# A decoder layer of attention, retention and mixture of experts: the weighing, the maxima and a quarter of the K projection at other places in the step

## The reference

```
x = layernorm(x + attention(x, Wqkv))         # 16 heads of 16, causal
x = layernorm(x + retention(x, ctx, Wq,Wk,Wv)) # xpos rotation, decay mask, no softmax
x = layernorm(x + moe(x))                      # one shared expert + top 2 of 8
```

## Time and profile before

| | us |
|---|---|
| median of 3 runs | 827.55 |
| lowest, highest | 826.76, 829.4 |
| the profiled execution, its own time | 829.99 |
| its span, first to last instruction | 828.2 |
| PE busy | 727.1 (88%) |
| DVE, ACT, POOL busy | 443.5, 385.3, 320.3 |
| K projection on PE | from 5.59 to 35.09 |
| scores of tile 0 start | 38.91 |
| steps 4 to 30, start of scores to start of scores of step 31 | 91.10 to 444.94 |
| first expert tile's transpose | 519.74 |

### The profile page before, as it was taken

The page is one execution under the profiler, slowest core; times in us unless marked ns, Lnnn a source line. Parts: engine busy times, 40 slices in busy tenths (PEclk is TensorE's granted clock), DMA queues, the critical chain, the costliest instruction groups (busy, mean ns, idle before and its releaser), DMA issues.

```text
span 828.2 us, 20209 instructions
## 1 busy us (share of the span) xinstructions
PE 727.1 (88%) x5972; PEld 539.4 (65%) x5973; DVE 443.5 (54%) x1506; ACT 385.3 (47%) x1105; POOL 320.3 (39%) x451
## 2 busy tenths in 40 slices
PE   7966898988989898898988864899999999999894
PEld 6745687877878787787877741466666666665453
DVE  3513555656556555656556563344444444446985
ACT  0055666766667666666667220233333333321333
POOL 1001222323443444444344666255555555550010
PEclk9969999999999999999999997899999999999998
DMA  8718441221322323232232545342222222227872
GB/s 306 260 31 241 148 134 52 67 77 52 92 78 79 95 62 103 67 90 77 79 98 81 173 123 181 99 145 85 87 83 89 84 88 83 89 70 253 283 257 77
DMA packets 77035, 97.69 MB, mean 118 GB/s; under 512 B 12320, under 2 KB 63264, under 8 KB 75936
## 3 DMA queue, kind: packets, MB, share of 16 engines
q1 hardware_dynamic: 59920, 68.31, 26.9%
q0 software_dynamic: 6816, 19.00, 6.5%
q10 hardware_dynamic: 10224, 9.42, 4.4%
HBM read 60.12 MB, written 36.56 MB: 117 GB/s over the span
## 4 chain that ended last, share of the span: by engine, by line
PE 71%; issue 12%; ACT 5%; DVE 4%; DMA 3%; POOL 3%; SPq 1%; ACTq 0%; POOLq 0%; DVEq 0%
PE ps L977 15%; PE ps L779 7%; PE ps L988 7%; ACT prob L1066 4%; PE ps L767 4%; PE ps L742 4%; PE ps L717 4%; PE ps L854 4%; PE ps L867 4%; PE ps L870 3%; PE ps L793 3%; PE ps L745 3%; PE ps L963 2%; PE ps L970 2%; PE ps L841 2%
## 5 line engine op out<-in xcount | busy, mean ns | idle before, releaser
L1066 ACT ACTIVATE prob<-ps,nmax 128x128 f32<-128x128 f32 x512 | 146.3, 377 | 2.6 <-DVE nmax L1229 1.8
L977 PE MATMUL ps<-first_use,xgT 128*128 x284 | 135.4, 600 | 1.5 <-ACT xgT L1163 1.5
L1229 DVE TENSOR_REDUCE nmax<-ps 128x4 f32<-128x512 f32 x128 | 86.3, 683 | 93.1 <-PE ps L767 93.1
L621 POOL TENSOR_TENSOR rot<-products 128x128 f32<-128x128 f32 x128 | 59.0, 481 | 186.9 <-DVE products L1239 186.9
L1073 ACT COPY pT<-ps 128x512 f32<-128x512 f32 x128 | 75.0, 586 | 88.0 <-PE ps L779 82.4
L1452 DVE TENSOR_TENSOR hid<-ps,attn_only 128x512 f32<-128x512 f32 x71 | 49.1, 692 | 101.6 <-PE ps L977 100.5
L1163 ACT COPY xgT<-ps 128x256 f32<-128x256 f32 x71 | 26.4, 372 | 140.9 <-PE ps L963 140.9
L670 POOL TENSOR_TENSOR gate_h<-hid,sil 128x256 f32<-128x256 f32 x71 | 50.7, 715 | 96.2 <-DVE result_row L1465 82.7
L779 PE MATMUL ps<-tf,prob 128*128 128x128 f32 x512 | 84.1, 289 | 3.3 <-ACT pT L1073 3.3
L1239 DVE TENSOR_TENSOR products<-ps,tf 128x256 f32<-128x256 f32 x128 | 48.4, 420 | 61.5 <-PE ps L870 44.1
L977 PEld LDWEIGHTS ps<-first_use,xgT 128*128 128x128 f32 x284 | 54.3, 192 | 40.4 <-issue 36.9
(11 more groups left out here) (133 smaller groups left out, 1352.5 us busy)
## 6 DMA issues: line engine op xcount, KB each, us to landing
xg<-sent ACTq DMA_DIRECT2D x68, 129.5 KB, 2.1
first_use<-back SPq DMA_DIRECT2D x8, 1024.0 KB, 8.2
k_dram<-first_use SPq DMA_DIRECT2D x4, 1024.0 KB, 6.0
attn_only<-in_x_turned SPq DMA_DIRECT2D x32, 128.0 KB
attn_only<-k_dram SPq DMA_DIRECT2D x256, 16.0 KB
attn_only<-in_x SPq DMA_DIRECT2D x32, 128.0 KB, 2.3
first_use<-in_L_ffn_rw SPq DMA_DIRECT2D x8, 512.0 KB, 5.7
attn_only<-in_ctx SPq DMA_DIRECT2D x32, 128.0 KB, 2.2
```

Source lines behind the costliest of these rows:

```text
L621: eng.tensor_tensor(rot[:, t % 2, m + e, :], ra[:, t % 2, m + e, :], rb[:, t % 2, m + 1 - e, :], ALU.add).then_inc(done, 1)
L977: mm = eng.matmul(ps[:, r, :], xgT[:, r, c, :], rw1_sb[:, bass.ds(e * (DC * 2 * FFN) + c * 2 * FFN, 2 * FFN)], start=(c == 0), stop=(c == ...
L1066: ins = eng.activation(prob[:, t % 2, 4 * u + n, :], SCORE[u][:, n * P:(n + 1) * P], ACT.Exp, bias=nmax[:, t % 2, 4 * u + n:4 * u + n + 1])
L1229: eng.tensor_reduce(nmax[:, t % 2, 4 * u:4 * u + 4], SCORE[u].rearrange("p (h j) -> p h j", j=P), AX_X, ALU.max, negate=True).then_inc(max ...
```

## The change

The eight weighing matmuls of each half become one block of 16 for tile n-2 at the start of step n, ahead of the scores. DVE takes all four maxima first and all of the gating last in its step; ACT's exponentials stand earlier, and the masks are laid last in PE's step, behind the x1 transposes. The retention's K and V come before its Q, SCX moves to bank 7 and YX behind the x2 transposes. POOL's step begins with x2b and the sends. Group 3 of the K projection moves into step 0 (three units) and step 1 (the fourth), with DVE's copies and SP's stores; SP waits only for the first store before it loads K. The weight loads begin at step 3. The diff, cut (repeated lines of moved blocks are left out):

```diff
-MAX_ORDER = (3, 0, 2, 1)
+MAX_ORDER = (3, 0, 1, 2)
...
-    return GROUPS[q][0] + GROUPS[q][1] + 5
+    return GROUPS[q][0] + GROUPS[q][1] + 4
...
-            if group_step(q) + 3 + (j if size == 4 else 0) == n]
+            if group_step(q) + 4 + (j if size == 4 else 0) == n]
...
-        SCX = ps[:, 6, 0:P]
+        SCX = ps[:, 7, 0:P]
...
-            for g in range(NG - 1):
-                store_k(g)
-
-            eng.wait_ge(k_stored[0], 16)
+            store_k(0)
...
                     if t < 2:
                         eng.wait_ge(consts_set, 2)
+                    if t == 0:
+                        eng.wait_ge(k_stored[0], 16)
...
-                    store_k(NG - 1)
-                if n == 1:
+                if n in (-1, 0, 1):
+                    store_k(n + 2)
+                if n == 3:
                     eng.wait_ge(k_stored[1], 16 * (NG - 1))
-                if 1 < n <= 1 + NE // 2:
+                if 2 < n <= 2 + NE // 2:
...
-                    for e in range(2 * (n - 2), 2 * (n - 1)):
+                    for e in range(2 * (n - 3), 2 * (n - 2)):
...
             def step(n):
-                t = n - 3
-                if live(t):
-                    turn_into(t, 2, pq_set, rot_q_set)
-                    turn_into(t, 0, pk_set, rot_k_set)
...
                 if n == 2:
                     eng.wait_ge(zeros_set, 1)
                     eng.dma_start(sent[IDLE_ROW:XROWS, :].rearrange("(n p) d -> p n d", p=P),
...
+                t = n - 5
+                if live(t):
+                    eng.wait_ge(x2_set, t + 1)
...
+                    eng.tensor_tensor(x2b[:, t % 2, :], packets[:, t % SLOTS, 0:D], sb2_sb[:, :], ALU.add).then_inc(x2b_set, 1)
                 for t in sent_at(n):
                     eng.wait_ge(pos_set, group_of(t) + 1)
                     for j in range(TOPK):
...
+                t = n - 3
+                if live(t):
+                    turn_into(t, 0, pk_set, rot_k_set)
+                    turn_into(t, 2, pq_set, rot_q_set)
...
+            def project_k(g, j, bank):
...
+                mm.then_inc(k_made, 1)
+            for g in range(NG - 1):
+                eng.wait_ge(xTu_in[g] if g else wk_in, 16)
+                    project_k(g, j, 4 + j)
+            eng.wait_ge(xTu_in[NG - 1], 16)
...
-            eng.wait_ge(kk_set, 4 * NG - 2)
+            eng.wait_ge(kk_set, 4 * NG - 5)
...
-                if t < 5:
+                if t < 4:
                     after(eng, q_set, t)
+                if t == 4:
+                    eng.wait_ge(pq_set, 2)
...
-            def weigh(t, u0):
-
-                eng.wait_ge(pT_set, t * 4 + u0 + 2)
...
+            def weigh(t):
+
+                eng.wait_ge(pT_set, t * 4 + 4)
+                eng.wait_ge(v_set, t + 1)
+                after(eng, att_set, t)
+                for h in range(H):
+                    lo = h % CG * VW
+                    mm = eng.matmul(HEADS_T[lo:lo + VW, h // CG, :], va[:, t % 3, h, :],
+                                    pT[:, h % 8 // 2, 2 * (h // 8) + h % 2, :], start=True, stop=True)
                 mm.then_inc(heads_made, 1)
...
+            def bank7_read(n):
+
+                eng.wait_ge(gc_set, min(n - 5, B))
+                for q in groups_at(n - 1, 3):
+                    eng.wait_ge(base_set, q + 2)
             def step(n):
-                if n == -1:
+                if n == 2:
                     eng.wait_ge(kk_set, 4 * NG)
+                if live(n - 2):
+                    weigh(n - 2)
                 if live(n):
                     scores(n)
+                if n == 0:
+                    eng.wait_ge(kk_set, 9)
+                    project_k(NG - 1, 0, 4)
+                if n == 1:
+                    eng.wait_ge(kk_set, 13)
                 if live(n - 1):
                     turn_probs(n - 1, 0)
+                if n == 1:
+                    eng.wait_ge(kk_set, 14)
+                    project_k(NG - 1, 3, 5)
+                t = n - 3
+                if live(t):
+
+                    eng.wait_ge(cT_in[t % 2], t // 2 * 16 + 16)
+                    eng.wait_ge(x1T_set, t + 1)
+                    for q in groups_at(n - 1, 3):
+                        eng.wait_ge(base_set, q + 2)
+                    for m in range(2):
+                        for c in range(DC):
...
+                    for c in range(DC):
+                        mm = eng.matmul(XV, cT[:, t % 2, c, :], xwv_sb[:, c, :], start=(c == 0), stop=(c == DC - 1))
+                    mm.then_inc(xkv_made, 1)
                 t = n - 2
                 if live(t):
 
@@ -840,10 +864,11 @@
                     for b in range(H // CG):
...
                     mm.then_inc(heads_turned, 1)
+                if live(n - 1):
+                    turn_probs(n - 1, 1)
                 t = n - 3
                 if live(t):
 
-                    eng.wait_ge(x1T_set, t + 1)
...
-                if live(n - 1):
-                    turn_probs(n - 1, 1)
...
-                if live(n - 1):
-                    turn_probs(n - 1, 2)
                 t = n - 4
                 if live(t):
...
                     if live(n - 3):
-                        eng.wait_ge(pq_set, 2 * (n - 3) + 2)
+                        eng.wait_ge(pk_set, 2 * (n - 3) + 2)
                     else:
-                        eng.wait_ge(res2_set, n - 4)
+                        bank7_read(n)
                     for m in range(2):
...
                     mm.then_inc(scx_made, 1)
                 if live(n - 1):
-                    weigh(n - 1, 0)
-                    turn_probs(n - 1, 3)
...
+                    turn_probs(n - 1, 2)
                 t = n - 5
                 if live(t):
 
...
-                    if live(n - 3):
-                        eng.wait_ge(pk_set, 2 * (n - 3) + 2)
+                    if live(n - 4):
+                        eng.wait_ge(scx_set, n - 3)
                     else:
-                        eng.wait_ge(gc_set, t)
+                        bank7_read(n)
...
                     mm.then_inc(x2_turned, 1)
+                t = n - 4
+                if live(t):
+                    eng.wait_ge(scx_set, t + 1)
+                    eng.wait_ge(xv_set, t + 1)
+                    if live(n - 3):
+                        eng.wait_ge(pq_set, 2 * (n - 3) + 2)
+                    else:
+                        eng.wait_ge(res2_set, t)
+                    eng.matmul(YX, scx[:, t % 2, :], xv[:, t % 2, :], start=True, stop=True).then_inc(yx_made, 1)
+                if live(n - 1):
+                    turn_probs(n - 1, 3)
-                if live(n - 1):
-                    weigh(n - 1, 2)
-                if live(n + 1):
-                    project(n + 1)
...
                     mm.then_inc(gate_made, 1)
                 if live(n + 1):
-                    lay_masks(n + 1)
-                for q in groups_at(n, 2):
+                    project(n + 1)
+                if n == 0:
+                    eng.wait_ge(kk_set, 12)
+                    project_k(NG - 1, 1, 5)
+                    project_k(NG - 1, 2, 7)
+                for q in groups_at(n, 3):
                     size = GROUPS[q][1]
...
                     mm.then_inc(x1_turned, 1)
+                if live(n + 1):
+                    lay_masks(n + 1)
...
-                after(eng, heads_made, 2 * t - 1 + u // 2)
+                after(eng, heads_made, t)
...
             def step(n):
+                t = n - 2
+                if live(t):
+                    eng.wait_ge(heads_made, t + 1)
+                    eng.copy(oT[:, :, :].rearrange("p x t -> p (x t)"), ps[:, 5, :]).then_inc(oT_set, 1)
+                if live(n - 1):
+                    out_probs(n - 1, 0)
+                if live(n):
+                    exps(n, 3)
                 for q in groups_at(n, 1):
...
-                if live(n - 1):
-                    out_probs(n - 1, 0)
-                if live(n):
-                    exps(n, 3)
-                if live(n - 1):
-                    out_probs(n - 1, 1)
-                if live(n):
-                    exps(n, 0)
                 t = n - 3
                 if live(t):
...
                     eng.copy(xv[:, t % 2, :], XV).then_inc(xv_set, 1)
+                if live(n):
+                    exps(n, 0)
                 if live(n - 1):
+                    out_probs(n - 1, 1)
                     out_probs(n - 1, 2)
-                    out_probs(n - 1, 3)
                 t = n - 5
...
                 if live(n):
+                    exps(n, 1)
                     exps(n, 2)
-                t = n - 1
-                if live(t):
-                    eng.wait_ge(heads_made, 2 * t + 2)
...
-                    eng.copy(oT[:, :, :].rearrange("p x t -> p (x t)"), ps[:, 5, :]).then_inc(oT_set, 1)
+                if live(n - 1):
+                    out_probs(n - 1, 3)
                 t = n + 1
...
```

(48 more changed lines are left out.)

108 lines of the change are left out of this document (34 added, 74 removed).

## The result

The changed kernel ran at **805.62 us** (median of 4 runs, 800.7 to 807.68) beside 827.55: ratio 0.9723, 95% interval 0.9674 to 0.9772. The forecast was 786 within 776 to 803, so the gain came out at half of the one forecast. The profiled run took 804.40 us, span 802.6 where before had 828.2.

What follows compares the result with a forecast made beforehand. PE, holding 71% of the span, was taken to bound the kernel, with its waits the rest. From 829.99 us, 24.9 (steady steps), 15.3 (start) and 1 (tail) gave 788.8, less 2.4 to the median: 786, range 776 to 803.

Steps and rivals of the forecast that it cites:

- Costed at nothing: Steady steps: gating's DVE work at the step's end and POOL's sends ahead of the rotations were given no cost.
- Steady steps: The 27 full attention steps: PE idle falls from 1.27 to about 0.35 us each, gain 24.9 us.
- the decay product's: Ordinary step, at the x2 transposes: PE newly waits 0.25 us for DVE's decay product.
- The PE work of a step is the same before and after ... so 319.46 us stay.: 27 steady steps: same matmuls and shapes, so PE's busy time is unchanged and only the waits change.
- Start: Up to step 4: scores(0) at 34, step 4 at 75.8 against 91.10, gain 15.3 us, bounds 6 and 20.
- the 11.52 us wait goes: Step 3: the first context tile no longer stands behind 2.4 MB of FFN weights on SP, so its 11.52 us wait disappears.
- cT(1) ... I take 0.5: Step 4: the second context tile now stands behind the weights; PE could stall 4.5 us, but 0.5 us was taken.
- A wait for cT(1) above 2 us: Listed sign of a wrong forecast: PE waiting more than 2 us for the second context tile.
- Rival A: Start: PE stands for K rows, the clock drops, steps 0 and 1 gain nothing; 795 us, chance 0.16.
- Tail: Weighing moved to step 33 costs 1.1 us, earlier sends save some 1.3, order changes about 1; gain 1, bounds -1 and 3.
- POOL sends first and then makes the rotations: Steady steps: sends and x2b sum end by about 3 us, K products come at 6.1, so no cost.
- B's 811: Step border: DVE's chain behind four maxima replaces the old wait in full, leaving start and tail gains; 811 us, chance 0.10.

Runs made afterwards that it cites:

- b1: Changed kernel with SP issuing the context tile and rows of x ahead of the expert weights, and POOL's sends last in its step: 772.11 us, ratio 0.9308.
- b2: Changed kernel with POOL's sends last, context tile and x rows ahead of the weights on SP, and weights started in step 2: 772.8 us, ratio 0.9341.
- z2: Changed kernel with the zero fill behind POOL's root of step 2 and the expert weights started in step 2, both as before the change: 779.12 us.
- e4: Changed kernel with the K projection whole in front again, as before the change: 783.44 us in one run.
- e1: Changed kernel with POOL's sends held until the first turn of probabilities: 774.34 us, ratio 0.9357.
- e2: Changed kernel with SP's K loads, not the sends, held until the first turn of probabilities in steps with sends: 773.85 us in one run.
- e3: Changed kernel with POOL's sends behind the reciprocal roots at the end of its step, as before: 771.67 us in one run, 774.85 when repeated.
- n1: Changed kernel with an always-over wait on POOL ahead of the sends, which holds nothing: 771.14 us in one run.
- n2: Changed kernel with an always-over wait on SP ahead of the K loads, which holds nothing: 772.12 us in one run.

## Why the forecast was wrong, step by step

What was gained in the three pieces, in the four measurements of the changed kernel (each against the row "before" of the first table):

| piece | forecast | first | second | third | fourth |
|---|---|---|---|---|---|
| up to scores(5) | 15.0 | 14.2 | 13.9 | 14.1 | 12.0 |
| steps 5 to 31 | 24.0 | 12.5 | 42.4 | 42.4 | 42.4 |
| behind scores(31) | 2.2 | -1.0 | -2.2 | -2.3 | -1.0 |
| span | 41.2 | 25.6 | 54.1 | 54.2 | 53.4 |

Two steps of the prediction failed, both in the middle piece. It put POOL's sends at the front of its step at nothing ("Costed at nothing"), and in the first measurement the steps with sends took 1.5 us more each; why then and not later stays open. And it kept PE's work of a step at the old 319.46 us, where the new order takes half a microsecond less a step.

**Steady steps: the mechanism right, the size too small.** In the three repeats the masks' wait is gone, the decay product's is there, and PE waits at no turn, as forecast. The whole list of PE's waits from step 5 to step 31 in the fourth measurement:

```profile
PE ps L905 <- DVE scx L1369: 5.1, 25, 0.2
```

The table of windows over these 26 steps:

```profile
91.91:390.52 298.61, 293.46 (x3841) 257.95 (x3837) 224.88 (x718) 222.49 (x682) 138.38 (x221) 1.00 0.34 98
```

Idle is (298.61 - 293.46)/26 = 0.20 us a step against the 0.35 that I took: with 1.27 before, 27.9 over 26 steps where I had 24.0. The larger miss is the sentence "The PE work of a step is the same before and after ... so 319.46 us stay." It is 293.46/26 = 11.29 a step against 319.46/27 = 11.83, 14.2 us over the 26. About 3 of the 14.2 are the clock: before had two steps like this one at a mean of 0.88, with 1.6 us more of PE work each than an ordinary one; the changed kernel had none in this stretch.

```profile
298.57:313.01 14.44, 13.28 (x147) 11.46 (x146) 7.98 (x27) 8.74 (x26) 5.55 (x9) 0.88 0.28 76
```

The rest shows in ordinary steps at full clock, 11.22 us of PE work, in this row of the fourth measurement, against 11.69:

```profile
137.64:149.07 11.43, 11.22 (x150) 9.89 (x146) 8.86 (x29) 8.65 (x27) 3.77 (x7) 1.00 0.24 72
```

Read by the distance of starts, the matmuls that shrank are those whose neighbours changed. First before, then the fourth measurement:

```profile
147.97 0.61 PE L884 MATMUL ps<-rot 128*128 128x128 f32 x4
148.51 0.64 PE L793 MATMUL ps<-pT,va 128*32 128x128 f32 x16
149.09 0.66 PE L779 MATMUL ps<-tf,prob 128*128 128x128 f32 x4
149.58 0.66 PE L894 MATMUL ps<-xv,scx 128*128 128x256 f32 x2
150.07 0.38 PE L906 MATMUL ps<-tf,packets 128*128 128x128 f32 x2
150.42 0.65 PE L793 MATMUL ps<-pT,va 128*32 128x128 f32 x16
151.00 1.16 PE L742 MATMUL ps<-attn_only 128*128 128x128 f32 x8
```
```profile
142.77 0.61 PE L892 MATMUL ps<-rot 128*128 128x128 f32 x4
143.24 0.63 PE L777 MATMUL ps<-tf,prob 128*128 128x128 f32 x4
144.07 0.41 PE L905 MATMUL ps<-tf,packets 128*128 128x128 f32 x2 [0.20 <-DVE scx L1369]
144.32 0.60 PE L916 MATMUL ps<-xv,scx 128*128 128x256 f32 x2
144.75 0.60 PE L777 MATMUL ps<-tf,prob 128*128 128x128 f32 x4
...
148.07 1.08 PE L787 MATMUL ps<-pT,va 128*32 128x128 f32 x32
149.08 1.17 PE L765 MATMUL ps<-attn_only 32*128 32x128 f32 x32
```

The weighing is one block of 1.01 us where two halves took 0.58 each, SCX 0.47, YX 0.43 and the x2 transposes 0.25 where they took 0.54, 0.49 and 0.35; that is 0.38 of the 0.47. The instruction counts are the same. That the cost lies in going from one form of matmul to another is an inference from these rows; no run isolates it. What the runs show is where it doesn't come from. Busy time per step, worked out from the windows from 91.09 to 380 us, is 269.65 of 288.91, or 11.75 of a mean step of 12.59, with the masks' order alone changed, and 255.78 of 288.91, or 11.33 of 12.80, with only the exponentials' order undone, both at a clock of 1.00: it goes with PE's order and not with the waits.

So a walk with PE's durations taken from their old neighbours was good to 0.5 us in 12, which is more than all the idle time that I left in a step.

**Start: the sum 1 to 3 us too good, and a reason misread.** scores(0) came at 32.7 to 34.2 (34 forecast), scores(4) at 77.5, 76.8, 74.8 and 74.7 in the four measurements (76.9), scores(5) at 89.7, 90.0, 89.8 and 91.9 (88.9). But "the 11.52 us wait goes" misread: a link of the chain that is a transfer's time from issue to landing is not what PE stood. PE's own row for it, above, says 3.1 us, and the mean clock of that step was 0.90. As the sum walks the new steps and takes nothing off for this wait, the misreading spoils the reason and not the number. And "cT(1) ... I take 0.5": the wait was 0.6, 1.6, 1.7 and 2.6 us in the four measurements, and step 4 took 12.2, 13.2, 15.0 and 17.2 where b1 and b2, without it, have 11.34. In the third and fourth the clock falls behind the wait and costs as much again; in the second, and in z2 with a wait of 2.55, it doesn't fall there. "A wait for cT(1) above 2 us" was on the list of what would show me wrong, and came in one of four. The Trainium skill (TensorE: Matmul & The Clock Gate, Part 1) has half rate as the default that activity lifts; the fourth measurement agrees, at K and XV of 2.08 and 1.92 us behind a wait.

Rival A (the clock lost at the start) came in three of four, at part of its price. Step 0 took 8.97, 11.11, 10.27 and 10.27 us, at a mean clock of 1.00, 0.76, 0.83 and 0.83: in the second measurement the scores ran at half speed (2.09 us), in the third and fourth the unit of the K projection behind them (3.67 us in the fourth, 1.99 in the first). Steps 0 to 2 together took 33.9, 31.7, 30.8 and 30.8 where before has 34.5; so the clock was lost in step 0 in the three repeats, and in steps 1 and 2 in the first measurement.

The move of a quarter of the K projection, which I had priced inside the start only, shows alone in e4: with it undone scores(31) start at 396.41, against 389.36, 388.47 and 387.92 in e1, e2 and e3 on the same chip, **7 to 8.5 us** later, and the whole took 783.44 us against 771.7 to 774.3. Four units are 7.4 us of PE by the earlier trace rows, so the move was worth about all of it. The expected text of e4 had it worth little: step 0 would be shorter by 5.5 us without the units and step 1 by 1.8. Measured against e1, step 0 is shorter by 1.8 only and step 1 longer by 4.1, as the rows of steps 0 and 1 show, first of e4, then of e1:

```profile
38.60:45.42 6.82, 3.57 (x60) 2.72 (x61) 2.48 (x4) 4.99 (x19) 0.79 (x1) 1.00 0.72 252
45.42:59.69 14.27, 10.81 (x109) 8.26 (x109) 2.48 (x4) 6.95 (x23) 0.00 (x0) 0.64 0.46 150
```
```profile
32.62:41.22 8.60, 8.60 (x85) 7.25 (x85) 4.83 (x7) 4.77 (x18) 0.50 (x1) 1.00 0.93 326
41.22:51.38 10.16, 8.25 (x133) 6.64 (x117) 4.29 (x6) 6.91 (x22) 0.00 (x0) 1.00 0.53 175
```

Without the units PE is busy for 3.57 of 6.82 us of step 0. So they mostly fill time in which it stood. Step 1 behind the thin step 0 then runs at a mean clock of 0.64, as it did before the change (0.57); with them it ran at 1.00 in e1 and 0.86 in the first measurement.

**Tail: a gain of 1 forecast, 1 to 2.3 lost.** The weighing that moved from step 32 to 33 is paid, as said. That POOL's sends would begin 1.3 us earlier doesn't show. Neither is certain: behind scores(31) the kernels of the four measurements, n1 and n2, the same there but for waits that hold nothing, took 381.2 to 385.6 us.

**The first measurement** lost 30 us in steps 12 to 31 (328.5 against 298.6). This is the step of the prediction that failed for the 805.62: "POOL sends first and then makes the rotations" was costed at nothing, and none of the rivals has it (B's 811 is near, but by a wait of PE that isn't there). Three repeats on three chips don't have it. It isn't known on which chip the first was made. A hold-up of signals while POOL issues indirect sends is what its rows look like; why there, and not in the same overlap elsewhere, stays open. The kernels that part sends and scores can't be called cures, since the changed kernel without them did as well. Against the three repeats (772.7 to 777.0) the forecast of 786 is 9 to 13 us too high, and its range just reaches them or just misses them.

## What to carry to other kernels

Ahead of pricing a reordering of PE, count its busy time as part of what the order decides: here the same matmuls in another order took 0.5 us less of a 12 us step, as much as many a wait. Take the length of a stall from the waits' own row and never from a transfer's link in the chain, and where a late transfer is only moved to another step, expect it to be late there. Where a step in the start gets longer with an edit, read its granted clock, and the same step in repeats of the unedited kernel, ahead of blaming the edit. When a changed kernel shows waits that no record explains, run the identical file again on other chips ahead of any cure.

## What the runs showed of the hardware

- The same file took 805.6 us in one measurement and 772.7 to 777.0 in three others, with the clock granted the same (0.975 against 0.967 to 0.971) and matmuls elsewhere of equal length. The difference lies wholly in 20 steps in which signals from PE reached ACT and DVE about 2 us late while POOL issued indirect sends, and were through 0.5 to 0.7 us behind the second of them.
- Late signals didn't touch the kernel before in that measurement, although its sends overlap the masks, the x1 transposes and the first scores of the next step (205.19 to 207.52 us, with its scores of step 13 from 207.31 at their full speed of 1.17 us).
- The granted clock after a stall isn't reproducible to the microsecond: behind waits of 1.6 and 1.7 us for the context tile step 4 lasted 13.2 and 15.0 us in two measurements of one kernel, and behind the wait for the K rows the scores of step 0 took 1.17 or 2.09.
- Nor is it in a step without a late transfer: step 2 of the same file took 13.14 us at a mean granted clock of 0.74 in one measurement and 10.38 at 1.00 in three.
- A zero fill from POOL's queue and K loads from SP's: scores(0) followed the last issue of the loads by 2.2 to 2.8 us where the fill's packets began at 31.8 to 32.2 us, and by 1.3 to 1.5 where they began at 32.5 or later.
